# Three of nine deformable-convolution taps taken by indirect DMA from a table of row pairs, in a four-block fused kernel

## What is computed

```python
off = jnp.einsum('nchw,oc->nohw', inputs, w_grid) + b_grid[None, :, None, None]
...
px = (gx + 1.0) * 0.5 * (W - 1)
py = (gy + 1.0) * 0.5 * (H - 1)
...
return tap(x0, y0, wx0 * wy0) + tap(x1, y0, wx1 * wy0) + tap(x0, y1, wx0 * wy1) + tap(x1, y1, wx1 * wy1)
...
out = jax.lax.conv_general_dilated(sampled, w_conv, window_strides=(k, k), padding='VALID', ...)
```

## Time and profile before

| what | us |
|---|---|
| median of 3 runs | 2190.97 |
| lowest, highest run | 2187.71, 2197.27 |
| span of the profiled execution | 2193.9 |
| TensorE matmul busy | 1908.1 (87%) |
| TensorE weight loads busy | 1640.2 (75%) |
| ScalarE busy | 1515.9 (69%) |
| VectorE busy | 1481.6 (68%) |
| GpSimd busy | 843.3 (38%) |

### The profile page before, as it was taken

How to read it: one execution, slowest core, us unless ns; L and a number is a source line. 1 busy time by engine, 2 the same in 40 slices (tenths; PEclk the granted TensorE clock), 3 DMA queues, 4 the chain that set the end, 5 groups by cost and what they waited for, 6 DMA issues and landing times.

```text
span 2193.9 us, 53330 instructions
## 1 busy us (share of the span) xinstructions
PE 1908.1 (87%) x20746; PEld 1640.2 (75%) x20746; DVE 1481.6 (68%) x3031; ACT 1515.9 (69%) x1787; POOL 843.3 (38%) x1626
## 2 busy tenths in 40 slices
PE   0248379999899999999899998999899999999999
PEld 0213277789777987789777997789777987789998
DVE  3147357975688757975688757976688656974544
ACT  0013257868686877867686877868686876869986
POOL 2000133344433543344433553345433643345554
PEclk9985589999999999999999999999999998999999
DMA  6744474558555764558555764558555763233331
GB/s 180 157 122 118 111 187 141 160 139 196 156 154 153 195 172 138 156 152 189 166 152 148 183 191 129 151 153 202 166 149 158 169 164 96 77 95 109 115 112 49
DMA packets 258765, 324.04 MB, mean 148 GB/s; under 512 B 201268, under 2 KB 212244, under 8 KB 254292
## 3 DMA queue, kind: packets, MB, share of 16 engines
q1 hardware_dynamic: 242948, 281.21, 46.9%
q0 software_dynamic: 3280, 29.86, 5.5%
q10 hardware_dynamic: 12288, 9.57, 1.5%
HBM read 251.21 MB, written 55.99 MB: 140 GB/s over the span
## 4 chain that ended last, share of the span: by engine, by line
PE 64%; DVE 18%; DVEq 6%; DMA 4%; issue 4%; SPq 2%; ACT 1%; ACTq 0%; POOL 0%; POOLq 0%
PE bank L1168 46%; PE bank L1267 5%; DVE strip L850 3%; DVEq L1034 3%; PE bank L1155 3%; PE bank L1225 3%; DVE code L1035 3%; DVE onehot L1042 3%; PE bank L1252 2%; PE bank L1143 2%; SPq L394 2%; DVE samp L857 1%; PE bank L1286 1%; DMA tent<-in_Wexp,expert 1%; DVE stats L778 1%
## 5 line engine op out<-in xcount | busy, mean ns | idle before, releaser
L1168 PE MATMUL bank<-picture,tent 128*128 128x160 f32 x9216 | 1380.2, 306 | 1.1 <-issue 0.6
L1168 PEld LDWEIGHTS bank<-picture,tent 128*128 128x128 f32 x9216 | 1290.5, 193 | 119.9 <-issue 53.4
L850 DVE TENSOR_TENSOR strip<-bank,near 128x480 f32<-128x480 f32 x768 | 498.5, 655 | 363.3 <-PE bank L1168 324.1
L560 POOL TENSOR_TENSOR strip<-strip 128x192 f32<-128x192 f32 x512 | 280.1, 547 | 1012.1 <-DVE strip L850 1010.1
L634 ACT ACTIVATE tent<-zs,row_at_sb 128x1152 f32<-128x1152 f32 x512 | 624.5, 1250 | 29.0 <-PE bank L1168 15.8
L638 ACT ACTIVATE tent<-tent 128x2304 f32<-128x2304 f32 x256 | 544.2, 2126 | 20.0 <-issue 1.1
L562 POOL TENSOR_TENSOR strip<-strip 128x96 f32<-128x96 f32 x512 | 242.8, 474 | 40.1
L566 POOL TENSOR_TENSOR samp<-strip 128x96 f32<-128x96 f32 x512 | 213.7, 417 | 57.5 <-POOL strip L562 0.9
L1267 PE MATMUL bank<-cb,xs 64*128 64x512 f32 x512 | 198.1, 709 | 23.1 <-DVE code L1035 15.4
L1033 DVE MAX8 top<-bank 128x8 f32<-128x512 f32 x256 | 175.6, 686 | 48.3 <-PE bank L1267 48.1
L623 ACT COPY samp_t<-bank 96x384 f32<-96x384 f32 x256 | 119.3, 466 | 106.4 <-PE bank L1155 85.3
(11 more groups left out here) (128 smaller groups left out, 1159.8 us busy)
## 6 DMA issues: line engine op xcount, KB each, us to landing
zs<-z_rows SPq DMA_DIRECT2D x256, 576.0 KB, 4.5
picked_weights<-arena SPq DMA_DIRECT2D x15, 1800.0 KB
arena<-picked_weights SPq DMA_DIRECT2D x24, 720.0 KB, 7.3
arena<-windows SPq DMA_DIRECT2D x288, 50.0 KB, 4.0
arena<-xp SPq DMA_DIRECT2D x96, 136.0 KB, 2.6
slice<-picked_weights SPq DMA_DIRECT2D x16, 720.0 KB, 6.3
windows<-arena SPq DMA_DIRECT2D x32, 312.5 KB, 5.5
slice<-windows SPq DMA_DIRECT2D x192, 50.0 KB, 3.1
```

Of the source, the lines that this page charges most:

```text
L560: pool.tensor_tensor(y[:, :, 0:2], y[:, :, 0:2], y[:, :, 2:4], ALU.add).then_inc(summing, 1)
L850: dve.tensor_tensor(y, STRIPS[J % 3][:, 0:DENSE * XW * C].rearrange("p (d c x) -> p d c x", d=DENSE, c=C), w.broadcast_to([128, DENSE, C, ...
L1168: m = pe.matmul(STRIPS[j % 3][:, XW * C * e:XW * C * (e + 1)], tent[:, N % TENTS, c, DENSE * d + e], picture[:, b % 2, i, c], start=(c == ...
```

## The change

Six of the nine taps go on as before; a tile now has two halves of three taps (`half(J)`, `HALVES`), with tents, `zs`, `near` and `z` for six taps. Half 0 is summed on GpSimd as before (three additions), half 1 by the reduction on VectorE. The last three taps of a tile are taken in another way:

- **The table.** `pairs_dram` holds for each image and each padded pixel (33 x 34 of them) 64 numbers: the 32 channels of the pixel and of the one below. Four consecutive corners (x, y), (x, y+1), (x+1, y), (x+1, y+1) are thus one run of 128 numbers (512 B). It is filled by four DMAs from ScalarE's queue in runs of 2 KB, four small DMAs from SyncE's (`pair_top`), and zero edges written once (`clear_edges`, on GpSimd's queue). `raw` is now loaded from this table (eight DMAs in place of four, 1280 B runs). TensorE makes 16 transposes of the image in place of eight, ScalarE copies four times in place of twice.
- **The positions.** `corners` on VectorE computes floors, fractions, four weights and one table index per pixel and tap (some 12 instructions in each front).
- **The fetch.** GpSimd issues three indirect DMAs per tile, each with 128 indices and 512 B per index, three tiles ahead (768 in all).
- **The weighing.** VectorE multiplies 128 x 384 fetched numbers by their weights (in place, both inputs in SBUF); GpSimd adds the four corners with two additions (128 x 192 and 128 x 96 results).

`PLACE` is recounted in halves: 5 beside each of the five rows, 1, 4, 2, 1, 2 from `features` to `norm2`, 20 beside the scores, 1, 1, 2 in `spell`, `pick`, `norm3`, and 2, 3 in `rows`, `near`; together 64; `SHIFT` is 14 halves, and 78 halves (39 tiles) are left after the last front.

The diff, cut to its core (the two functions `half` are GpSimd's and VectorE's; then TensorE's wait and ScalarE's writes to the table):

```diff
-THIRDS = 3
-DENSE = TAPS // THIRDS
+HALVES = 2
+DENSE = 3
+STRUNG = HALVES * DENSE
+FETCHED = TAPS - STRUNG
...
+            def fetch(N):
...
+                if n == 0:
+                    pool.wait_ge(corner_ready, b + 1)
+                    pool.wait_ge(pairs_out[b % 2], 16 * 4 * (b // 2 + 1))
+                    pool.wait_ge(top_out[b % 2], 16 * 4 * (b // 2 + 1))
...
+                if N >= FETCHES:
+                    pool.wait_ge(gathered, N - FETCHES + 1)
+                for k in range(FETCHED):
+                    at = FETCHED * (TILES * i + t) + k
+                    pool.indirect_dma_start(fetched[:, N % FETCHES, k].rearrange("p q c -> p (q c)"), None,
+                                            pairs_dram[b % 2],
+                                            bass.IndirectOffsetOnAxis(ap=corner[:, b % 2, at:at + 1], axis=0)
+                                            ).then_inc(fetched_in[N % FETCHES], 16)
...
+            def half(J):
+                N, d = divmod(J, HALVES)
+                if d == 0:
+                    y = strip[:, d]
+                    pool.wait_ge(strip_read, J + 1)
+                    pool.tensor_tensor(y[:, :, 0:2], y[:, :, 0:2], y[:, :, 2:4], ALU.add).then_inc(summing, 1)
...
                     return
...
+                y = fetched[:, N % FETCHES]
+                pool.wait_ge(weighed, N + 1)
+                pool.tensor_tensor(y[:, :, 0:2], y[:, :, 0:2], y[:, :, 2:4], ALU.add).then_inc(gathering, 1)
...
+                pool.tensor_tensor(samp[:, N % 2, PARTK * 2:PARTK * 3].rearrange("p (k c) -> p k c", c=C),
+                                   y[:, :, 0], y[:, :, 1], ALU.add).then_inc(gathered, 1)
+                fetch(N + FETCHES)
...
+            def half(J):
...
+                if d == 0 and N > 0:
+                    dve.wait_ge(summed, N)
...
+                if d == 0:
+                    y = fetched[:, N % FETCHES].rearrange("p k q c -> p (k q) c")
+                    at = FETCHED * (TILES * i + t)
+                    w = share[:, b % 2, at:at + FETCHED].rearrange("p k x y -> p (k x y)").unsqueeze(2)
+                    dve.wait_ge(fetched_in[N % FETCHES], 16 * FETCHED * (N // FETCHES + 1))
+                    dve.tensor_tensor(y, y, w.broadcast_to([128, FETCHED * CORNERS, C]), ALU.mult).then_inc(weighed, 1)
                     return
...
             def turn_samples(N):
                 pe.wait_ge(samp_ready, N + 1)
-                pe.wait_ge(summed, 2 * (N + 1))
+                pe.wait_ge(summed, N + 1)
+                pe.wait_ge(gathered, N + 1)
...
+                dst = pairs_dram[g % 2]
+                for r in range(4):
+                    act.dma_start(bass.AP(dst.tensor, dst.offset + 2 * C * (IMG * TX + EIGHTH * r + 1),
+                                          [[IMG * TX * 2 * C, H], [TX * 2 * C, IMG], [1, EIGHTH * 2 * C]]),
+                                  pairs[r:128:4].rearrange("p i n y c -> p i (n y c)")).then_inc(pairs_out[g % 2], 16)
```

More of the change, by code:

```diff
@@ L403, in at @@
                 def at(name, first=0, end=None):
-                    for J in thirds_at(g, name, first, end):
-                        third(J)
+                    for J in halves_at(g, name, first, end):
+                        half(J)
                 full = MOST * C // PATCHES
@@ L480, in _ @@
                 front(g)
-            for J in range(LEFT, THIRDS * ALL):
-                third(J)
+            for J in range(LEFT, HALVES * ALL):
+                half(J)
             store(GROUPS - 1, 1)
@@ L571, in _ @@
                 pick_weights(0, h)
+            for h in range(2):
+                clear_edges(h)
             for g in range(GROUPS):
@@ L595, in _ @@
                 subtract(g)
-                at("near", 0, 4)
+                at("near", 0, 2)
                 clip(g)
-                at("near", 4)
-            for J in range(LEFT, THIRDS * ALL):
-                third(J)
+                at("near", 2)
+                if g == 0:
+                    for N in range(FETCHES):
+                        fetch(N)
+            for J in range(LEFT, HALVES * ALL):
+                half(J)
         @engines.scalar
@@ L668, in at @@
                 def at(name, first=0, end=None):
-                    for J in thirds_at(g, name, first, end):
-                        third(J)
+                    for J in halves_at(g, name, first, end):
+                        half(J)
                 if k and k >= KEPT:
                     load_x(k)
-                at("row0", 0, 4)
+                at("row0", 0, 3)
                 if k:
                     root(k, 0)
-                at("row0", 4)
+                at("row0", 3)
                 for v in range(1, NV - 1):
@@ L804, in _ @@
             dve.memset(xp0[:], 0.0)
+            dve.memset(fetched[:, 0], 0.0)
             dve.drain()
```

341 lines of the change are left out of this document (204 added, 137 removed).

## The result

The changed kernel takes **2309.51 us** (median of four runs, 2308.2 to 2311.25) against 2193.22 (four runs, 2187.71 to 2197.27) for the kernel before: a ratio of 1.053, with a 95% interval of 1.050 to 1.056. It is 5.3% slower; 2275 us and slower had been forecast, by the mechanism that ranked first. The profiled execution has a span of 2308.6 us.

What follows compares the result with a forecast made beforehand. GpSimd was to bound R and the tail at T = 6.83 us a tile; first part, six periods and tail sum to 1380 + 131.5 T = 2278 us of span, 2275 us median, 4% slower; range 2110 to 2400.

Steps and rivals of the forecast that it cites:

- the mechanism that ranked first: GpSimd bounds the kernel at about 1.3 to 1.45 us a fetch, giving 2200 to 2330 us; chance 0.47.
- R: Stage of a period with offsets, `rows`, `near` and five rows of patches: from 101.7 us to 110.9, set by GpSimd.
- the tail: Part after the six periods, 240.6 us before: forecast 294.3 us, with 41.5 tiles at GpSimd's pace.
- S: Stage of a period from scores to `norm3`: from 108.0 us to 102, with VectorE full.
- T: GpSimd's time for one tile: 6.83 us from sums of 1.64 and 1.03 and fetches of 4.16; bounds 4.26 to 7.65.
- the back-to-back pair: Two adjacent indirect DMAs in the earlier trace, 1.37 us from start to start, taken to price each tile's three fetches.
- The descriptor rule: GpSimd can't write DMA descriptors during VectorE's two-port modes; some 5 us a front, 30 us more in all, left out.
- M: Stage of a period from `features` to `norm2`, a chain of small steps: stays at 39.7 us.
- rival 2: In R and the tail, an indirect DMA costs under 1.17 us with its gap; whole 2134 or 1978 us; chance 0.26.
- even point: GpSimd's tile time at which the change neither gains nor loses: 6.19 us, or 1.17 us per indirect DMA, gap included.
- rival 3: The fetch or the shared port costs more, 7.4 to 8.2 us a tile on GpSimd: 2350 to 2460 us; chance 0.19.
- What was costed at nothing: Table writes, edges, `raw` loads and eight more transposes hide in R; DMA share there at most 0.9; fetch landing hidden.

Runs made afterwards that it cites:

- run 1: Changed kernel with the third of each tile's three indirect DMAs left out, weighing and additions kept: 2148.82 us.
- run 3: Changed kernel with each indirect DMA replaced by a plain one of the same shape, issued at the same point by GpSimd: 2104.27 us.
- run 4: Changed kernel without VectorE's weighing; GpSimd waits for the fetch itself and adds unweighted numbers: 2237.01 us.
- run 5: Changed kernel with the four fetched corners summed by one VectorE reduction in every tile, in place of two GpSimd additions: 2219.1 us.
- run 9: Changed kernel with both GpSimd sums made VectorE reductions in R and the tail only: 2079.48 us once, then 2067.77 us, ratio 0.943 to the kernel before.
- run 6: Changed kernel with one of each tile's three indirect DMAs issued behind the next tile's strip sum, order alone: 2318.74 us.
- run 7: Changed kernel with two slots for the fetches in place of three, so fetches run two tiles ahead: 2346.45 us.

## Why the prediction was right, and where its terms were off

**The mechanism.** GpSimd's length of a tile decides, in R and in the tail. The chain (38% of it GpSimd) and the tail tile show it, and so do the runs 1, 3, 4, 5 and 9, each of which shortens GpSimd's program in another way and gains (in run 4 the part that S gained is VectorE's). The forecast's bounds of T were wide (4.26 to 7.65); choosing the back-to-back pair of the earlier trace rows over the plain issues of the earlier trace rows was the step on which the sign hung, and it rested on one pair at the start of the kernel. Had an indirect issue cost what a plain one does, the change would have gained 4% (run 3).

**T, 6.83 forecast, 6.84 measured, by luck: two errors of 0.4 us cancel.** The issues were put at 4.16 us and take 3.77 (0.27 + 0.96 + 0.30 + 0.95 + 0.30 + 0.95, and 0.04 of rounding in the starts): from start to start they are 1.26 apart, not 1.37, because an issue takes 0.95 and not 1.07 as the first of the pair in the earlier trace rows did; 128 indices cost no more than 100 did, and the gap of 0.31 was real. The sums were put at 2.67 and take 3.07, 0.39 of it in L635: this is the port, which the prediction had named and priced at 0.4 to 0.6 us, but left out of the sum and kept for the range. It belonged in the sum: L627 sets off both GpSimd's L631 and L635 and, through L938, the next tile's weighing, and both sides take 0.7 us from there, so that L635 and a weighing meet in nearly every tail tile (36 of 42). The prediction's sign for this, a weighing far above 0.6 us, watched the wrong side: the weighing's mean is 0.550 us, and GpSimd's addition is what got longer.

**The descriptor rule.** Some indirect issues do get longer beside VectorE, but few. GpSimd's timeline and VectorE's, in stage R:

```profile
1007.41 1.15 DVE L1236 SCALAR_TENSOR_TENSOR near<-near 128x960 f32<-128x960 f32 x1
```

```profile
1007.74 1.64 POOL L583 DMA_INDIRECT fetched<-row_pairs,corner  x1 [0.30 <-issue]
```

This issue began inside an operation of VectorE that still had 0.82 us to go and took 1.64 us, 0.69 more than the usual 0.95. Over all 768 the mean is 976 ns and the shortest 940, so everything of this kind costs at most 768 x 0.036 = 28 us of GpSimd's time. Issues of over 1.05 us are 54 of the 768, and all but two of them overlap either an operation of VectorE with two inputs in SBUF (L1236, L1165, the weighing L945 and others, 40) or the normalisation L885, which has one (12). The 27 issues that began inside a weighing took 1.11 us on average. The plain issues of run 3 behave otherwise: the 35 that began inside a weighing took 0.55 us on average, as all did, while seven beside the same normalisation took 0.65 to 0.99 in place of 0.54. So a weighing delays only the indirect form, which also has indices to read from SBUF (`corner`); whether that is the reason was not tried. The Trainium skill, page "SBUF — State Buffer", section "SBUF: two separate sides", has the rule that GpSimd can't write descriptors while VectorE runs an operation in a two-port mode; the plain issues beside the normalisation fit it (0.99 us at most in place of 0.54) if that operation runs in such a mode, which no run here tells. By it the sum had been 30 us higher, 2305, nearer to the 2309.5 measured. That nearness proves little: by the rule the issues would be dearer than forecast, and with all excess and idle time ahead of them they took (749.6 + 247.1) / 256 = 3.89 us a tile, 0.27 less than the 4.16 forecast.

**The stages.** R: 106.0 against 110.9, M: 47.1 against 39.7. Read together: 153.1 against 150.6. GpSimd's backlog passes from R into M: in the trace GpSimd finishes 14 or 15 tiles in R and 6, not 5, in M, and 6 x 6.84 = 41 us is more than the 39.7 forecast for M. The step that failed is "the chain of small steps stays: 39.7". Part of it is that the one period that I read in windows was not a typical one (the mean of five is M 42.0); the rest is the fetches themselves: M is 47.1 with three, 44.8 with two, 41.8 with none. S: 104.6 against 102; I had given back two thirds of VectorE's 13 us of gaps, and the window still has 15.0 (106.7 - 91.7). Even without any fetch S is 103.4, so the gaps are not the fetches' doing. Period: 256.8 against 252.6; the six make 25 of the 30.6 us that the span lies above the forecast's 2278. The first part, left at 468.6, is 474.5 and makes 6: with two fetches or none it is 466 to 467, so in the front of group 1 GpSimd already counts. The tail came out as forecast, 293.3 against 294.3. TensorE was busier than forecast, 80.3 us in R (75) and 68% of the tail (56%): its matmuls had been priced at the full clock, and the granted one was 0.93 and 0.90. It was not the bound in either.

**`corners`** was put at 3 us a front and is 5.8 (46.4 over eight fronts). Two of its groups by line, and its longest instruction on VectorE's timeline:

```profile
L964 DVE SCALAR_TENSOR_TENSOR place<-floors 128x96 f32<-128x96 f32 x8 | 9.9, 1238 | 0.0
L970 DVE TENSOR_SCALAR corner<-place 128x24 uint32<-128x24 f32 x32 | 6.6, 270 | 0.0
...
1001.94 1.97 DVE L964 SCALAR_TENSOR_TENSOR place<-floors 128x96 f32<-128x96 f32 x1
```

This fits the port again: that L964 has both its inputs in SBUF, began 0.18 us after GpSimd's `near` of 2.04 us, and ended 0.11 us after it.

```profile
1001.76 2.04 POOL L607 TENSOR_TENSOR near<-pos,column_at_sb 128x960 f32<-128x960 f32 x1
```

It stands in R, where VectorE has room.

**The rivals.** The cheap indirect issue (rival 2) falls: 1.26 us is above the even point of 1.17, if only by 8%. With what the runs show the even point is lower still: the span would have to fall by 115 us at 130 us for each of T, to T = 5.96, which is (5.96 - 3.07) / 3 = 0.96 us for an issue. The dearer fetch (rival 3) falls too: T grows by the port as it said, but its 7.4 needed issues that cost as much as forecast. What was costed at nothing stayed hidden: no line of the table's writes or of the transposes is among the first of the chain, and the DMA share in R is 0.80 against at most 0.9. The landing stayed hidden.

## What to carry to other kernels

Before work is handed to an engine that looks idle on average, add up its program for one round, instruction by instruction and with the gaps between issues, and compare that with the round time that the other engines would reach without it; an engine busy for 38% of the span became the bound because it got 3.8 us of issues in each 6.8 us. When an engine is the bound by its total work, moving its instructions about gains nothing (run 6); taking work away from it does, and pays most where the receiving engine has room in that very stage: run 5 put one sum on VectorE everywhere and S grew by 7.8 us (2219 us in all), run 9 put both there in R and the tail alone and S did not grow (2068 us). When one event sets off work on two engines, that work meets in every round at the same distance; follow both sides from the event, and if they come to a shared port together, its price belongs in the sum and not in the range. And when a view gives a landing time for a tile, look which transfers it counts.

## What the runs showed of the hardware

An indirect DMA of 128 indices with 512 B each holds GpSimd for 0.95 us, and the next one starts 0.30 us after its end; a plain one of the same shape holds it for 0.54 with no gap (run 3). The three fetches of a tile have landed 3.4 us (median, an estimate from semaphore updates) after the start of the last issue, but after 11.4 to 15.4 us when they stand behind a larger indirect DMA on the same queue, which is late enough to show with two slots (run 7). An operation of VectorE with two inputs in SBUF makes an indirect issue that starts inside it longer (1.11 us on average inside a weighing, 1.67 at most), and left the plain issues of run 3 as they were (0.55).

TensorE's granted clock was lower in stretches in which TensorE waited longer: 0.84 in the window of M, against 1.00 before, and 0.90 in the tail, against 0.98 in the tail of run 9, in which TensorE waits little. The timeline of TensorE in M:

```profile
1140.35 3.41 PE L1287 MATMUL bank<-picture,tent 128*128 128x160 f32 x12
```

Twelve products take 3.41 us here; 36 took 4.89 before, 1.63 for twelve, so these ran at the lower of the two levels, 1.2 GHz. Ahead of them, but for three transposes, TensorE had waited 4.04 us. A kernel in which another engine becomes the bound thus also gets a slower TensorE: in the tail its busy time is 199.4 us for the same 1425 matmuls that take 173.7 us in run 9. In this tail TensorE stands idle for the other 94 us, so no run shows that the lower clock cost time.
